# Two-layer transformer, attention of the first layer: the second head's softmax product moves to GpSimd, and queries' and keys' rotary sums become one

## The reference

```python
def _rope(x, sin, cos):
    xe = x[..., ::2]
    xo = x[..., 1::2]
    re = xe * c - xo * s
    ro = xe * s + xo * c
    return jnp.stack((re, ro), axis=-1).reshape(x.shape)

def _attn(xq, ctx, wq, wkv, wo, bo):
    ...
    q = _rope(q, sq, cq)
    k = _rope(k, sk, ck)
    sim = jnp.einsum('bhnd,bhmd->bhnm', q, k) * DH ** (-0.5)
    a = jax.nn.softmax(sim, axis=-1)
    o = jnp.einsum('bhnm,bhmd->bhnd', a, v)
    o = o.transpose(0, 2, 1, 3).reshape(xq.shape[0], xq.shape[1], MID)
    return o @ wo + bo
```

## Time and profile before

| | |
|---|---|
| three runs, us | 404.35, 403.86, 403.36 (median 403.86) |
| profiled execution, us | 404.24, of it the span from first to last instruction 402.4 |
| TensorE clock granted | 1.0 of full speed over the whole span |
| busy, us | matmuls 381.1, weight loads 285.1, VectorE 320.5, ScalarE 296.7, GpSimd 141.9 |
| sines (L298) | 62 of 1283 ns mean |
| products (L715) | 64 of 773 ns mean |
| sums (L737) | 64 of 700 ns mean |

### The profile page before, as it was taken

One profiled execution on the slowest core, in us unless ns is written; L12 is line 12 of the kernel. 1 busy time (PEld: TensorE's weight loads), 2 busy tenths in 40 slices (PEclk: granted clock), 3 DMA queues, 4 the chain that ended last, 5 costly groups with the idle time before them and its releaser, 6 DMA issues.

```text
span 402.4 us, 9925 instructions
## 1 busy us (share of the span) xinstructions
PE 381.1 (95%) x3604; PEld 285.1 (71%) x3604; DVE 320.5 (80%) x702; ACT 296.7 (74%) x1031; POOL 141.9 (35%) x126
## 2 busy tenths in 40 slices
PE   7979999999999999999999998999999999999997
PEld 3557767777777777777777667776768777787664
DVE  4998998988998898989898858673658888788740
ACT  2277886886887777878788795779679787987832
POOL 4364423423634333734245324430264620202010
PEclk9999999999999999999999999999999999999999
DMA  7133333332333233331212110000000000000001
GB/s 230 41 122 115 117 119 99 118 108 100 110 108 132 87 116 113 105 107 55 105 53 80 67 43 26 2 2 1 2 2 3 0 2 4 2 2 2 2 0 54
DMA packets 17348, 25.71 MB, mean 64 GB/s; under 512 B 3630, under 2 KB 6068, under 8 KB 17300
## 3 DMA queue, kind: packets, MB, share of 16 engines
q1 hardware_dynamic: 16548, 24.07, 17.7%
q10 hardware_dynamic: 720, 1.00, 0.8%
q0 software_dynamic: 32, 0.00, 0.0%
HBM read 8.28 MB, written 0.52 MB: 22 GB/s over the span
## 4 chain that ended last, share of the span: by engine, by line
PE 52%; DVE 18%; ACT 17%; issue 9%; POOL 2%; POOLq 0%; DVEq 0%
PE bank L947 41%; ACT prob L424 8%; PE bank L1034 6%; DVE qk L737 4%; PE bank L1242 4%; ACT raw L516 3%; DVE prob L715 2%; DVE qk L728 2%; DVE nmax L825 2%; POOL xn L279 1%; DVE xn L651 1%; PE bank L958 1%; ACT raw L415 1%; POOL rstd L272 1%; DVE x L631 1%
## 5 line engine op out<-in xcount | busy, mean ns | idle before, releaser
L298 POOL TENSOR_TENSOR swp<-swp,small 128x512 f32<-128x512 f32 x62 | 78.9, 1283 | 129.6 <-PE bank L947 96.9
L424 ACT ACTIVATE prob<-bank,nmax 128x128 f32<-128x128 f32 x256 | 91.4, 390 | 1.2 <-DVE nmax L708 1.2
L516 ACT ACTIVATE raw<-bank,nmax 128x128 f32<-128x128 f32 x256 | 72.9, 391 | 11.6 <-DVE nmax L825 11.3
L424 ACT ACTIVATION_READ_ACCUMULATOR prob<-bank,nmax 128x1 f32 x256 | 59.1, 231 | 0.0
L825 DVE TENSOR_REDUCE nmax<-bank 128x4 f32<-128x512 f32 x64 | 41.1, 684 | 17.4 <-PE bank L947 17.4
L708 DVE TENSOR_REDUCE nmax<-bank 128x4 f32<-128x512 f32 x64 | 41.2, 685 | 16.2 <-PE bank L947 16.2
L715 DVE TENSOR_TENSOR prob<-prob,rz 128x512 f32<-128x512 f32 x64 | 49.4, 773 | 2.2
L947 PE MATMUL bank<-hT,wqkv 128*128 128x512 f32 x96 | 49.1, 595 | 0.3 <-DVE qk L728 0.3
L430 ACT ACTIVATE probT<-bank 128x512 f32<-128x512 f32 x32 | 19.1, 597 | 38.4 <-PE bank L1034 38.4
L1034 PEld LDWEIGHTS bank<-small,prob 128*128 128x128 f32 x256 | 28.5, 140 | 26.1 <-DVE prob L715 16.8
L272 POOL TENSOR_TENSOR rstd<-vare,neg_half 128x4 f32<-128x4 f32 x12 | 12.4, 1031 | 95.9 <-DVE vare L643 95.8
(11 more groups left out here) (111 smaller groups left out, 635.5 us busy)
## 6 DMA issues: line engine op xcount, KB each, us to landing
swp<-raw SPq DMA_DIRECT2D x124, 128.0 KB, 2.0
wqkv<-in_wqkv SPq DMA_DIRECT2D x14, 256.0 KB, 3.0
wff<-in_wff SPq DMA_DIRECT2D x4, 256.0 KB, 3.0
x<-in_x SPq DMA_DIRECT2D x2, 256.0 KB, 5.3
wqkv<-in_wqkv ACTq DMA_DIRECT2D x2, 256.0 KB, 5.7
wmod<-in_wmod SPq DMA_DIRECT2D x2, 256.0 KB, 2.8
ctx<-in_ctx SPq DMA_DIRECT2D x1, 384.0 KB, 7.4
ctxT<-in_ctxT SPq DMA_DIRECT2D x1, 384.0 KB, 3.5
```

The source lines that it names most:

```text
L298: nc.gpsimd.tensor_tensor(four(swp[:, m % 2, f, :]), four(swp[:, m % 2, f, :]), sin[f], ALU.mult).then_inc(rope_sin[f], 1)
L424: last = nc.scalar.activation(prob[:, hh, bcols(u)], S[hh][:, bcols(u)], ACT.Exp, bias=nmax[:, s % 2, hh, u:u + 1], accum_out=zsum[:, s % ...
L516: last = nc.scalar.activation(prob1[:, s % 2, hh, bcols(u)], score_bank(s, hh)[:, bcols(u)], ACT.Exp, bias=nmax[:, s % 2, hh, u:u + 1])
```

## The change

In the first layer GpSimd makes the product of head 1 (`normalise_second`) with the reciprocal that VectorE still computes (`invert_sums`); VectorE keeps head 0. The reciprocal of head 1 stands right behind the sums in the same item, where it stood, with its product, at the end of the item's background. The sums of queries and keys are one instruction of 1024 columns with one semaphore `roped`. On GpSimd the product of item s - 1 stands ahead of the wait for the scores of item s and of the sines; the power of items 11 and 19 moves one item on. In item 30 the one sum stands ahead of head 0's product, where the keys' sum stood behind it.

```diff
@@ -177,8 +177,9 @@
-        filled, raw_out, rope_cos, rope_sin, roped, first_swap, first_sin = (
-            pair(name) for name in ("filled", "raw_out", "rope_cos", "rope_sin", "roped", "first_swap", "first_sin"))
+        filled, raw_out, rope_cos, rope_sin, first_swap, first_sin = (
+            pair(name) for name in ("filled", "raw_out", "rope_cos", "rope_sin", "first_swap", "first_sin"))
+        roped = sem("roped")
         swapped = [pair(f"swapped_{name}") for name in ("q", "k")]
@@ -214,7 +215,7 @@
                     if m >= 2:
-                        sp.wait_ge(roped[f], m - 1)
+                        sp.wait_ge(roped, m - 1)
                     for e in range(2):
@@ -328,7 +329,16 @@
+            def normalise_second(s):
+                pool.wait_ge(recips[1], s + 1)
+                nc.gpsimd.tensor_tensor(four(prob[:, 1, :]), four(prob[:, 1, :]),
+                                        rz[:, s % 2, 1, :].unsqueeze(2).broadcast_to([P, HALF, P]), ALU.mult).then_inc(
+                    norms[1], 1)
             def l0_slot(s):
+                if s >= 1 and s != 30:
+                    normalise_second(s - 1)
                 if 0 <= s < ITEMS - 2:
@@ -339,9 +349,8 @@
                     context_inv_std(s - 1)
-                if s in (11, 19):
+                if s in (12, 20):
                     inv_std(s // RUN - 1, 1)
-                if s in (12, 20):
                     normalise_first(s // RUN - 1, 1)
@@ -351,6 +360,7 @@
                 if s == 29:
+                    normalise_second(29)
                     rope_sine(ITEMS - 1, 0)
@@ -363,8 +373,9 @@
             pool.wait_ge(ld_tab, 16)
-            for s in range(-1, ITEMS):
+            for s in range(ITEMS):
                 l0_slot(s)
+            normalise_second(ITEMS - 1)
             for j in range(1, SLOTS):
@@ -708,13 +719,17 @@
-            def normalise(s, hh):
+            def invert_sums(s, hh):
                 dve.wait_ge(exps[hh], s + 1)
                 nc.vector.reciprocal(rz[:, s % 2, hh, :], zsum[:, s % 2, hh, :]).then_inc(recips[hh], 1)
-                dve.wait_ge(recips[hh], s + 1)
-                nc.vector.tensor_tensor(four(prob[:, hh, :]), four(prob[:, hh, :]),
-                                        rz[:, s % 2, hh, :].unsqueeze(2).broadcast_to([P, HALF, P]), ALU.mult).then_inc(
-                    norms[hh], 1)
+            def normalise(s):
+                invert_sums(s, 0)
+                dve.wait_ge(recips[0], s + 1)
+                nc.vector.tensor_tensor(four(prob[:, 0, :]), four(prob[:, 0, :]),
+                                        rz[:, s % 2, 0, :].unsqueeze(2).broadcast_to([P, HALF, P]), ALU.mult).then_inc(
+                    norms[0], 1)
@@ -728,25 +743,23 @@
-            def rope_sum(m, f):
-                if m:
-                    dve.wait_ge(rope_sin[f], m)
-                else:
-                    dve.wait_ge(first_sin[f], 1)
-                dve.wait_ge(rope_cos[f], m + 1)
-                nc.vector.tensor_tensor(qk[:, m % 2, f, :], qk[:, m % 2, f, :], swp[:, m % 2, f, :], ALU.add).then_inc(
-                    roped[f], 1)
+            def rope_sum(m):
+                for f in range(2):
+                    if m:
+                        dve.wait_ge(rope_sin[f], m)
+                    else:
+                        dve.wait_ge(first_sin[f], 1)
+                    dve.wait_ge(rope_cos[f], m + 1)
+                nc.vector.tensor_tensor(qk[:, m % 2, :, :], qk[:, m % 2, :, :], swp[:, m % 2, :, :], ALU.add).then_inc(
+                    roped, 1)
...
                 rope_cosine(0, f)
-                rope_sum(0, f)
             def l0_slot(s):
-                if s >= 1 and s != 30:
-                    normalise(s - 1, 1)
                 row_max(s, 0)
@@ -754,15 +767,15 @@
                     copy_T0(s - 1)
+                if s == 30:
+                    ln_normalise(3, 0)
                 shift0(s)
                 if s == 30:
-                    ln_normalise(3, 0)
-                    rope_sum(31, 0)
-                normalise(s, 0)
-                if s + 1 < ITEMS:
-                    if s != 30:
-                        rope_sum(s + 1, 0)
-                    rope_sum(s + 1, 1)
+                    rope_sum(31)
+                normalise(s)
+                if s < 30:
+                    rope_sum(s + 1)
+                invert_sums(s, 1)
                 if s + 2 < ITEMS:
@@ -806,7 +819,6 @@
                     rope_cosine(ITEMS - 1, 1)
-                    normalise(29, 1)
                     residual(2, 0, O, acc_done[0], 1)
@@ -845,8 +857,6 @@
             def l1_slot(s):
-                if s == 0:
-                    normalise(ITEMS - 1, 1)
                 if s < ITEMS:
@@ -932,6 +942,7 @@
             first_rope(0)
+            rope_sum(0)
             context_stats(0)
@@ -1007,10 +1018,10 @@
             def score(s):
-                for f in range(2):
-                    pe.wait_ge(roped[f], s + 1)
-                    if s:
-                        pe.wait_ge(exps[f], s)
+                pe.wait_ge(roped, s + 1)
+                if s:
+                    for hh in range(2):
+                        pe.wait_ge(exps[hh], s)
                 if s == 29:
```

## The result

The changed kernel takes 404.81 us (median of 20 runs, 403.73 to 407.2), the kernel before 403.61 (20 runs on the same chip, 402.77 to 404.45): ratio 1.0032 [1.0021, 1.0042], 0.3% slower. The profiled executions stand closer: 404.41 us with a span of 402.6, against 404.24 and 402.4.

What follows compares the result with a forecast made beforehand. TensorE (381.1 of 402.4 us busy) was taken as the bound, VectorE mattering only where TensorE waits; - 1.5 + 1.3 + 0.8 = + 0.6 on 403.86 gave 404.5 us. Own range 403.3 to 405.6, with most of two rivals 402.3 to 406.6.

Steps and rivals of the forecast that it cites:

- Plain items: About twenty items where nothing waits: change 0, the product hidden by the score matmuls with 0.29 us to spare.
- the sum of 1024 columns: On VectorE, one sum replaces two of 512 columns: 1.22 us estimated instead of 1.28, bounds 1.13 and 1.28.
- The product on GpSimd: Second head's product, taken as 1.27 us from GpSimd's sine product, bounds 1.03 and 1.56; VectorE took 0.69.
- Rival 1: GpSimd's product is longer or handed over later, so transposes wait in more items: at 1.56, 406.8 us; chance 0.20.
- The four late items: Items 2, 4, 6, 8, where transposes wait for VectorE's chain: 4 x 0.38 = 1.5 us won.
- Item 20's 0.42: Item 20 gains 0.42 us as items 2, 4, 6, 8 do; together with item 21, 0.16 lost.
- Items 13, 21 and 28: GpSimd's layer norm rows precede its product: 0.42 lost in 13, 0.72 in 28, 0.16 in 20 and 21; together 1.3 us.
- Rival 2: GpSimd and VectorE avoid each other: xn slips between VectorE's product and sum, km is not held; 402.0 us, chance 0.17.
- The masked keys: Layer's end: VectorE's km meets GpSimd's last product and delays layer 1's first scores by 0.8 us; other end 0.28, or 0.
- the 0.97 row: VectorE's product at 257.86 took only 0.97 under GpSimd's one-input mask, 0.28 more, against the whole-instruction exclusion rule.
- Item 30, "I take 0": The one sum delays the first head's product by 0.5 us, but the next transposes come at about the same moment: 0.
- Rival 3: Gains vanish because the sines' transfers set the pace: + 2.1, 406.0 us; chance 0.10.

Runs made afterwards that it cites:

- order_only: Kernel before, both products on VectorE, with only the second head's reciprocal and product moved right behind the two sums: 401.86 us, ratio 0.9954.
- four_on_vector: Changed kernel with the second products of items 12, 20, 27 and 31 back on VectorE, the other 28 on GpSimd: 401.74 us, ratio 0.9950.
- two_pieces: Changed kernel with every sum in two instructions of 512 columns, one semaphore raised only by the second: 403.73 us, ratio 0.9996.
- extra_wait: Changed kernel with one more wait per item on TensorE, same semaphore and count, holding nothing up: 403.05 us, ratio 0.9969 to the kernel before.

## Why the prediction was right, and where not

The forecast was 404.5 us, from +0.6 on the kernel before; the profiled executions differ by 0.17, the medians by 1.2. The number fell in place, but partly for reasons that were not in it.

*Plain items and the sum of 1024 columns.* Right: length unchanged, 1.22 as estimated.

*The product on GpSimd.* Mis-sized: 1.27 assumed from the sine, 1.04 measured over 32 of them, next to the lower bound, the power's 1.03. Both are two-input ops of 128 x 512; the sine's broadcast operand repeats over the four batches, the reciprocal's along the row. The runs don't show which property makes the difference. Rival 1 (1.56) fell with it.

*The four late items.* Right in kind: 1.29 won where 1.5 was forecast, the waits gone. Item 20's 0.42 came too. What it rests on is the order, as `order_only` shows.

*Items 13, 21 and 28.* Right in mechanism, too dear in two of three: together 1.3 forecast after item 20's gain, 0.90 measured (3 x 0.44 - 0.42). The 0.23 that the product is shorter is nearly all of item 28's 0.28. Item 13's 0.42 came as 0.44 by two errors: the product was 0.23 shorter, and the two layer norm rows ended 0.71 after the scores' start (109.64 + 2.28 = 111.92, against 111.21), where the forecast had 0.38 (112.6, against 112.22). `four_on_vector` confirms the place. Rival 2's slip of the layer norm rows between VectorE's work did not happen.

*The masked keys.* Right that they meet the product: 1.00 for 0.48, and 0.36 more from item 31's scores to layer 1's, where 0.8 was forecast. The product is shorter than assumed, and the keys did not wait for all of it: 256.61 + 1.04 = 257.65, and the keys, alone 0.48, end at 257.93, so they began to run some 0.2 before the product's end. The rule of the Trainium skill, page "SBUF — State Buffer", section "Who interferes with whom", on exclusion for the whole instruction, fits this trace nearly; the 0.97 row still stands against it.

*Item 30, "I take 0".* Wrong: +0.32. The keys' sum ahead of the first head's product holds that product; the seven kernels run with both sums ahead of it there have 6.17 to 6.56, those with the keys' sum behind it 5.86 to 5.91. So the keys' sum ahead of that product has a cost of its own, apart from the fetches.

*Not seen at all.* The fetches of TensorE's code, which the missing wait moved. They go with longer items in the kernel before too: its item 5, whose late sine was read as the transfers' own pace, won 0.67 where its fetch went elsewhere. By the ratios, 1.0032 against 0.9969, their place costs 2.5 us, more than any term of the sum; by the medians, 1.8. Without that cost the change would have been a gain of 1.3 us, where the sum has + 0.6: item 5 and items 12 and 19 gave what was not counted, and the shorter product made items 21, 28 and the masked keys cheaper. Two errors cancelled, so that the number came out right is in part luck. Rival 3 said that the sines' transfers set the pace, worth + 2.1; this is what happened in items 1 and 7, by a cause that the rival did not name. The forecast's own range is slightly off too: with the masked keys at 0 and the product at 1.03 in the three items its lower end is 404.5 - 0.8 - 3 x 0.24 = 403.0, not 403.3.

*What stays open.* Of the 2.5 us the profiled executions show 1.2 (402.6 against 401.4). The rest is not located in any trace: the changed kernel's runs spread over 3.5 us, those with the extra wait over 0.9. Item 1 is 7.4 to 7.5 long with queue 8's fetch at 22.2 to 22.4 or at 27.5 us; queue 14's fetch goes with it, but no run moved that one alone with the one sum kept. Nor was it found what gives `two_pieces` its 0.36%; VectorE's program, longer there by an instruction per item, is one candidate that was not tried by itself.

## What to carry to other kernels

Price an edit on the instruction stream of the busiest engine too, also a wait that goes: its code is fetched by transfers too, and in this kernel 32 waits on TensorE, one per item, went with 0.4% of the median and 0.6% of the ratio. Before a change of under 1% is believed or dropped, time it once with a harmless wait added or taken. Order and engine are two edits: here the second head's place ahead of the background gave the gain, and GpSimd's product was free in the plain items, where nothing else stood ahead of it on GpSimd.

## What the runs showed of the hardware

A product of 128 x 512 in f32 with a reciprocal repeated along the row takes GpSimd 1.04 us, VectorE 0.69; GpSimd's sine product of the same size 1.27. A code fetch of TensorE is one packet of 16 KB and took 0.9 to 1.8 us, 29 or 30 times in the execution. With one beside a weight transfer of 256 KB in item 7, that landed after 4.2 us (3.8 to 4.3 in five kernels) instead of 2.7. VectorE's one-input op of 512 columns under a GpSimd two-input product takes 1.00 us instead of 0.48 (the changed kernel and `extra_wait` alike).
